# Context loads ahead of the row loads that wait, a slot's rows split ahead of its weight pieces with three homes for the transposes, and all slot loads issued by SyncE

## The reference, cut to what matters

```python
si = ctx @ W[:, :256][0];  sj = ctx @ W[:, 256:][0]          # per batch
xattn = 0.6 * sigmoid(si[:, :, None] + sj[:, None, :] + b) + 0.4 * layernorm(x)
x = x + tanh(g_xattn) * xattn
xt = layernorm(x).reshape(4096, 1024)
probs = softmax(xt @ wg);  e = argmax(probs);  gate = probs[e]
x = x + tanh(g_ffn) * gate * (xt @ W_ffn[e].T + b_ffn[e])     # one expert per token
```

## Time and profile before

| | |
|---|---|
| Median of 3 runs | 746.28 us (744.73 to 748.25) |
| The profiled execution: its own time, its span | 753.2 us, 751.5 us |
| TensorE, VectorE, GpSimd, ScalarE busy | 78%, 57%, 44%, 37% of the span |
| Granted TensorE clock, mean | 0.87 of full speed |
| First stage, until the last router product | 0 to about 222 us |
| Slot products, first to last | 259.8 to 737.9 us, 36 slots |
| DMA | 134.5 MB, 179 GB/s on average |

### The profile page before, as it was taken

How to read it: one execution, slowest core, us unless ns; L and a number is a source line. 1 busy time by engine, 2 the same in 40 slices (tenths; PEclk the granted TensorE clock), 3 DMA queues, 4 the chain that set the end, 5 groups by cost and what they waited for, 6 DMA issues and landing times.

```text
span 751.5 us, 13383 instructions
## 1 busy us (share of the span) xinstructions
PE 582.9 (78%) x2841; PEld 468.4 (62%) x2842; DVE 431.0 (57%) x555; ACT 275.6 (37%) x408; POOL 333.5 (44%) x488
## 2 busy tenths in 40 slices
PE   6798384668870199977977998797798799949992
PEld 5566263456660187856865887586587578738882
DVE  4377171538867887377278257457537735673341
ACT  3576243337741433233233233233324323332221
POOL 2467272637862333533533532532543254236552
PEclk9599586869995599988998999898899789979996
DMA  7803343516768886586586549648537745725552
GB/s 274 343 2 131 123 142 112 196 59 221 231 240 269 225 223 200 158 224 196 165 224 196 170 143 237 188 144 244 173 126 201 216 158 156 193 85 172 165 169 62
DMA packets 83718, 134.48 MB, mean 179 GB/s; under 512 B 11584, under 2 KB 64320, under 8 KB 83648
## 3 DMA queue, kind: packets, MB, share of 16 engines
q1 hardware_dynamic: 46496, 59.83, 27.5%
q10 hardware_dynamic: 27360, 40.17, 19.3%
q0 software_dynamic: 9792, 33.82, 11.3%
HBM read 99.97 MB, written 35.91 MB: 181 GB/s over the span
## 4 chain that ended last, share of the span: by engine, by line
issue 21%; PE 21%; DVE 20%; ACTq 10%; ACT 8%; DMA 7%; POOL 6%; DVEq 2%; SPq 2%; POOLq 2%
PE pair L970 9%; DVE wt L720 7%; ACT wt L532 4%; PE pair L897 3%; DVE pair L715 3%; PE pair L908 3%; DMA table<-xr,pos 3%; DMA ctx_in<-in_ctx 3%; ACTq L261 3%; DVE xr L656 3%; DVE rows L741 2%; PE pair L881 2%; DVE scatter_row L738 2%; PE pair L886 2%; ACTq L584 1%
## 5 line engine op out<-in xcount | busy, mean ns | idle before, releaser
L970 PE MATMUL pair<-wt,xt 128*128 x1728 | 421.8, 408 | 88.5 <-DVE xt L732 56.2
L970 PEld LDWEIGHTS pair<-wt,xt 128*128 128x128 f32 x1728 | 342.0, 199 | 168.0 <-issue 94.4
L424 POOL TENSOR_TENSOR rows<-rows,rb 128x1024 f32<-128x1024 f32 x37 | 88.1, 2382 | 185.0 <-ACT rb L551 185.0
L732 DVE TENSOR_TENSOR xt<-pair,xt 128x1024 fp32r<-128x1024 f32 x38 | 46.3, 1218 | 87.9 <-ACT xt L538 87.7
L532 ACT ACTIVATE wt<-pair 128x1024 f32 (+1 forms) x64 | 64.5, 1025 | 80.3 <-DVE pair L715 72.8
L715 DVE STREAM_TRANSPOSE pair<-w_raw 128x1024 f32<-128x1024 f32 x64 | 78.4, 1248 | 25.1 <-issue 24.0
L720 DVE TENSOR_TENSOR wt<-pair,wt 128x1024 f32 (+1 forms) x64 | 77.6, 1212 | 23.6 <-ACT wt L532 23.6
L538 ACT ACTIVATE xt<-pair 128x1024 fp32r<-128x1024 f32 x38 | 39.0, 1026 | 102.5 <-issue 49.8
L728 DVE STREAM_TRANSPOSE pair<-xb 128x1024 f32<-128x1024 f32 x38 | 47.8, 1259 | 44.2 <-issue 24.5
L551 ACT ACTIVATE rb<-bias_bc,scal 128x1024 f32 (+1 forms) x37 | 46.0, 1244 | 54.9 <-POOL scal L421 43.0
L908 PE MATMUL pair<-xc_tr,wg_sb 128*8 128x128 f32 x512 | 64.9, 283 | 0.0
(11 more groups left out here) (120 smaller groups left out, 452.9 us busy)
## 6 DMA issues: line engine op xcount, KB each, us to landing
w_raw<-in_L_ffn_W SPq DMA_DIRECT2D x256, 128.0 KB, 3.2
rows<-table ACTq DMA_DIRECT2D x38, 520.0 KB, 4.2
xb<-table ACTq DMA_DIRECT2D x152, 128.0 KB, 2.6
xr<-in_x SPq DMA_DIRECT2D x32, 512.0 KB, 6.0
ctx_in<-in_ctx SPq DMA_DIRECT2D x8, 512.0 KB, 4.7
bias_bc<-in_L_ffn_b SPq DMA_DIRECT2D x8, 512.0 KB, 4.4
out_x<-rows,scatter_row POOLq DMA_INDIRECT x36, 4.0
rows<-table SPq DMA_DIRECT2D x1, 520.0 KB, 5.5
```

The source lines that it names most:

```text
L424: nc.gpsimd.tensor_tensor(rows[:, k, 0:H], rows[:, k, 0:H], rb[:, :], ALU.add).then_inc(base_ready, 1)
L732: nc.vector.tensor_tensor(xt[:, k, 1, :, :].rearrange("p k n -> p (k n)"), ps[:, :], xt[:, k, 0, :, :].rearrange("p k n -> p (k n)").bitca ...
L970: last = nc.tensor.matmul(out_ps[r % 2][:, HALF * h:HALF * (h + 1)], xt[:, r % 2, x_part, k, :], wt[:, bass.ds(par, 1), w_part, k, HALF * ...
```

## The change

It has four parts. (1) SyncE issues context groups 4 to 7 ahead of all x tiles from 16 on. (2) In a slot, rows t + 2 are transposed first and cut behind the first piece's transpose, and the slot is finished last; `xt` has three homes. (3) SyncE issues all table loads and weight pieces in a loop of its own, and ScalarE none; `rows` has three buffers (`RING` = 3) and each loop is unrolled six times (`TURN` = 6), so `SLOTS` is 42. One number, `work`, tells what a slot does: 1 rows alone, 2 the first slot of an expert (pieces 0 to 3), 3 the slot behind it (pieces 4 to 7), 4 both. (4) Between the stages the order is new, and `finished` is raised early. The rest makes room in SBUF: `ones`, `after_start` and two others lie in tensors of the first stage. The core of the diff, in the order of the file: sizes, SyncE, ScalarE, VectorE between the stages, VectorE in a slot.

```diff
 
     Q, NB, QW = 4, 4, H // 4
...
-    RING = 4
...
-    TAB = SLOTS + RING
+
+    RING = 3
...
+            for g in range(4, NG):
+                sp.wait_ge(ctx_turned, g - 1)
+                sp.dma_start(ctx_in[:, g % 2, :], group_of(ctx_t, g)).then_inc(ctx_landed[g % 2], 16)
             for t in range(RX, T):
-                if t % GR == 0 and t // GR < NG:
-                    g = t // GR
-                    sp.wait_ge(ctx_turned, g - 1)
-                    sp.dma_start(ctx_in[:, g % 2, :], group_of(ctx_t, g)).then_inc(ctx_landed[g % 2], 16)
                 sp.wait_ge(row_stored[slot_of(t)], 16)
                 sp.dma_start(xr[:, slot_of(t), 0:H], tile_of(x_t, t)).then_inc(x_landed[slot_of(t)], 16)
...
-            load_rows(sp, 0, 0, 0)
-            for n in range(K, E * K):
-                e, m = n // K, n % K
-                sp.wait_ge(w_turned, n - WR + 1)
-                load_piece(e, m)
-                if m == WR:
-
-                    sp.wait_ge(w_ready, K * e + 1)
-                    sp.dma_start(bias_bc[:, e % 2, :], bias[e:e + 1, :].to_broadcast([P, H])).then_inc(bias_landed, 16)
+            load_blocks(sp, 0, 0)
+            load_rows(sp, 0, 0)
+            sp.wait_ge(slots_told, 1)
...
+            load_blocks(sp, row_of(1), 1)
+            load_rows(sp, row_of(1), 1)
+            sp.wait_ge(xb_turned, 1)
+            load_blocks(sp, row_of(2), 2)
+            for m in range(WR):
+                sp.wait_ge(w_turned, K - WR + m + 1)
+                load_piece(1, m)
+
+            with sp.Fori(0, SLOTS // TURN) as i:
+                for r in range(TURN):
+                    t = TURN * i + r
+                    work = sp.value_load(slot_tab[0:1, 0, bass.ds(t, 1)], min_val=0, max_val=4)
+                    with sp.If(work > 0):
+                        sp.wait_ge(xb_turned, t + 2)
+                        load_blocks(sp, row_of(t + 3), r + 3)
+                        if r == 0:
...
+                            sp.wait_ge(out_stored[(r - 1) % RING], 32 * i + 16 * ((r - 1) // RING + 1))
+                        load_rows(sp, row_of(t + 2), r + 2)
+                        with sp.If(work > 2):
+
+                            before = sp.value_load(slot_tab[0:1, 3, bass.ds(t, 1)], min_val=0, max_val=E - 2)
+                            with sp.If(before < E - 2):
+                                e = sp.value_load(slot_tab[0:1, 3, bass.ds(t, 1)], min_val=0, max_val=E - 3)
+                                for m in range(WR):
+                                    sp.wait_ge(w_turned, K * e + K + WR + m + 1)
+                                    load_piece(e + 2, m)
+                            with sp.Else():
+                                sp.nop()
+                            sp.nop()
+                        with sp.Else():
+                            sp.nop()
...
+                        with sp.If(work > 1):
+                            with sp.If(odd < 1):
+                                e = sp.value_load(slot_tab[0:1, 1, bass.ds(t, 1)], min_val=0, max_val=E - 2)
+                                for m in range(WR, K):
+                                    sp.wait_ge(w_turned, K * e + K + m - WR + 1)
+                                    load_piece(e + 1, m)
+
+                                sp.wait_ge(w_ready, K * e + K + 1)
+                                sp.dma_start(bias_bc[:, bass.ds((e + 1) % 2, 1), :].rearrange("p a h -> p (a h)"),
+                                             bias[bass.ds(e + 1, 1), :].to_broadcast([P, H])).then_inc(bias_landed, 16)
+                            with sp.Else():
...
-            next_rows(1, 1, 0)
-            xt_high(0, 0, cut_b)
             cut_high(0, 4, 0, cut_a)
             cut_high(0, 5, 0, pair[1])
-            exp_sum(0, 0)
+            xt_high(0, 0, cut_b)
             cut_high(0, 6, 0, cut_a)
             cut_high(0, 7, 0, pair[1])
+            exp_sum(0, 0)
             scaled_bias(0, 0, 0, 0)
...
+                    with act.If(work > 0):
+
+                        settled(summed, t + 1)
+                        xt_high(t + 2, (r + 2) % RING, cut_a)
                         exp_sum(t + 1, (r + 1) % RING)
-                    with act.Else():
-                        act.nop()
...
+                        with act.If(work > 2):
+                            last_pieces()
...
+                        odd = act.snap(work % 2)
+                        with act.If(work > 1):
+                            with act.If(odd < 1):
+                                first_pieces()
...
                         e1 = act.value_load(slot_tab[0:1, 1, bass.ds(t + 1, 1)], min_val=0, max_val=E - 1)
                         scaled_bias(t + 1, (r + 1) % RING, e1, act.snap(e1 % 2))
-                        next_rows(t + 3, (r + 3) % RING, i + (r + 3) // RING)
-                        settled(summed, t + 2)
-                        xt_high(t + 2, r, cut_a)
...
             position(NG - 1)
...
+            dve.sem_inc(finished, 2)
+            turn_weights(0, 2, cut_a, 2)
+            turn_weights(0, 3, pair[1], 3)
...
             cut_low(0, 3, 0, pair[1])
+            turn_weights(0, 4, cut_a, 4)
+            turn_weights(0, 5, pair[1], 5)
+            cut_low(0, 4, 0, cut_a)
             turn_rows(0, 0, 0, cut_b)
-            turn_weights(0, 4, cut_a)
+            cut_low(0, 5, 0, pair[1])
+            turn_weights(0, 6, cut_a, 6)
             xt_low(0, 0, cut_b)
-            turn_weights(0, 5, pair[1])
-            cut_low(0, 4, 0, cut_a)
...
             xt_low(1, 1, cut_b)
-
-            dve.sem_inc(finished, 2)
...
                         for m in range(first, first + K // 2):
-                            turn_weights(e, m, (cut_a, cut_b)[m % 2])
-                            if m > first:
-                                cut_low(e, m - 1, par, (cut_a, cut_b)[(m - 1) % 2])
-                        cut_low(e, first + K // 2 - 1, par, cut_b)
+                            turn_weights(e, m, (cut_b, cut_a)[m % 2], m - first)
+                            if m == first:
+                                behind_first()
+                            else:
+                                cut_low(e, m - 1, par, (cut_b, cut_a)[(m - 1) % 2])
+                        cut_low(e, first + K // 2 - 1, par, cut_a)
                         settled(w_ready, K * e + first + K // 2)
 
...
+                    def rows_cut(t=t, home=home):
+                        xt_low(t + 2, home, cut_a)
+                        dve.wait_ge(xt_ready, t + 3)
+
+                    with dve.If(work > 1):
+                        rows_turned()
+                        with dve.If(work > 2):
+                            last_pieces(rows_cut)
+                            with dve.If(work > 3):
+                                first_pieces(lambda: None)
+                            with dve.Else():
+                                dve.nop()
+                            dve.nop()
+                        with dve.Else():
+                            first_pieces(rows_cut)
+                        finish(t, r)
...
+                        with dve.If(work > 0):
+                            rows_turned()
+                            xt_low(t + 2, home, cut_a)
+                            finish(t, r)
```

More of the change, by code:

```diff
@@ L737, in finish @@
                 settled(base_ready, t + 1)
-                nc.vector.tensor_tensor(scatter_row[:, r:r + 1], rows[:, r, TOK:TOK + 1].bitcast(I32),
+                s = r % RING
+                nc.vector.tensor_tensor(scatter_row[:, s:s + 1], rows[:, s, TOK:TOK + 1].bitcast(I32),
                                         beyond[:, bass.ds(t, 1)], ALU.max)
                 settled(summed, t + 2)
-                nc.vector.scalar_tensor_tensor(out=rows[:, r, 0:H], in0=out_ps[r % 2][:, :], scalar=scal[:, r, 7:8],
-                                               in1=rows[:, r, 0:H], op0=ALU.mult, op1=ALU.add).then_inc(finished, 1)
-            turn_weights(0, 0, cut_a)
+                nc.vector.scalar_tensor_tensor(out=rows[:, s, 0:H], in0=out_ps[r % 2][:, :], scalar=scal[:, s, 7:8],
+                                               in1=rows[:, s, 0:H], op0=ALU.mult, op1=ALU.add).then_inc(finished, 1)
+            turn_weights(0, 0, cut_a, 0)
             for h in range(2):
                 dve.wait_ge(xc_copied[h], T)
-            turn_weights(0, 1, pair[1])
+            turn_weights(0, 1, pair[1], 1)
             cut_low(0, 0, 0, cut_a)
@@ L751, in _ @@
             position(NG - 1)
-            turn_weights(0, 2, cut_a)
-            turn_weights(0, 3, pair[1])
+            dve.sem_inc(finished, 2)
+            turn_weights(0, 2, cut_a, 2)
+            turn_weights(0, 3, pair[1], 3)
             cut_low(0, 2, 0, cut_a)
@@ L861, in _ @@
             for n in range(8):
-                nc.tensor.matmul(pair[1][:, 0:P], ones[:, :], ones[:, :], start=True, stop=True)
+                nc.tensor.matmul(pair[1][:, 0:P], ones, ones, start=True, stop=True)
             pe.wait_ge(masks_ready, 1)
```

(10 more changed lines are left out.)

222 lines of the change are left out of this document (117 added, 105 removed).

## The result

The changed kernel takes **689.05 us** (median of 4 runs, 688.07 to 693.0), the kernel before 747.08 beside it: a ratio of 0.9237, 95% interval 0.9193 to 0.928. In a second comparison on another chip, with the kernel before at 750.22, it took 687.3, ratio 0.9187 (0.9104 to 0.927). The forecast was 657, with a range of 628 to 692. The direction is right and the time is inside the range, but the gain is 58 us and not 89.

What follows compares the result with a forecast made beforehand. TensorE's waits for context loads and for `xt_low` behind VectorE's long turns, plus slow clock, bound it: 753.2 - 40 - 3 - 50.4 + 4 = 663.8 on the profiled execution, less 6.9 to the median: 657 us, range 628 to 692.

Steps and rivals of the forecast that it cites:

- code loading in every long turn: Rival: each of 12 long turns behind slot 3 costs 3 us more for instruction fetch; 693 us, chance 0.1.
- the rival with the port always lost: Slots: VectorE's finish always waits for GpSimd's addition, h = 18.1 us; 682 on the profiled execution, 675 us; chance 0.23.
- Part 1, tiles: Tile stage: TensorE's three waits for context loads go, with some slow products; -40 us, bounds -30 and -46.
- Part 2, passage: Between the stages: TensorE may start near 248 instead of 259.8 us, which brings little by itself.
- Part 3: Slots: one TensorE wait of 2.4 us per expert plus 2.0 slow clock; -50.4 us, first change another -3.
- h: Length of one long VectorE turn, a slot that prepares weights, from finish to finish; taken as 17 us.
- The dead heat at the port: In a long turn, row numbers and GpSimd's addition start together; h = 15.9 or 18.1 us, the middle, 17, taken.
- the rule of the Trainium skill: GpSimd and a two-SBUF-input VectorE operation share a port in turn; the later is blocked for the other's whole length.
- The low part of the rows now covers ScalarE's 1.3 us.: Long turn: VectorE's wait of 1.3 us for ScalarE ahead of the first cut is hidden behind the rows' low part.
- VectorE wins the port: Rival, slots: row numbers start before GpSimd's addition, h = 15.9 us, TensorE's wait shrinks to 0.2; 629 us, chance 0.2.
- Part 4, queues: ScalarE loses five DMAs a slot, hidden, nothing counted; SyncE's 21 issues make 9.5 us in a turn of 17.
- Part 5, loops: Returns to the loop's head in longer loops +3 us (0 to 6), two more empty slots at the end +1; +4.

Runs made afterwards that it cites:

- the context alone: The kernel before with only the context loads moved ahead, slots as before: 708.93 us, ratio 0.9438 to the kernel before.
- the run with the late count: The changed kernel with the count of finished slots raised late again, behind the setup of slots: 691.63 us, ratio 0.917 to the kernel before.
- the port alone: The changed kernel with VectorE's row-number operation moved from the turn's end to behind the rows' low part: 677.93 us, ratio 0.9035 to the kernel before.
- the kernel with the sum last: The changed kernel with ScalarE's exponent sum behind the high parts of the pieces instead of ahead of them: 671.47 us, ratio 0.8939 to the kernel before.
- the longer body: The changed kernel with 12 slots in the loop's body instead of 6, and 36 slots in all instead of 42: 678.21 us, ratio 0.9053.

## Why the prediction was right, and where it wasn't

**Sum against sum**, on the spans of the profiled executions, 751.5 and 687.3 us: -64.2, forecast -89.4. To slot 3: 296.73 to 252.94, -43.8 (forecast -40 - 3). Slots 3 to 30: 373.0 to 348.3, -24.7 (forecast -50.4, and +3 for the returns). The last six: 68.0 to 67.8. From the last product to the end: 13.7 to 18.3, +4.6 (forecast +1). So 22.7 of the 25 us of error are in the third stretch, slots 3 to 30, and 3.6 at the end. That 689 lies inside the range is partly luck: its upper end stood for code loading in every long turn (693 us), and the rival with the port always lost came to 675.

**Part 1, tiles: right.** -40 forecast; the last router product ended at 184.2 instead of 221.8, -37.6, with 5 us lost ahead of tile 4 (in the second profile at 180.8); with the context alone, the first slot product came 41.1 earlier. x tile 16 wasn't late.

**Part 2, passage: right.** First product forecast at 208, measured 211.2 and 207.2. That starting early brings little by itself is what the run with the late count showed.

**Part 3, the step that failed: the length of a long turn.** The formula held: wait = 1.3 + 2h - 32.9. The turns of t = 4 and 5, 13 and 14, 17 and 18, 22 and 23, 27 and 28 took 36.0, 36.1, 38.4, 35.2 and 36.7 us in pairs, which by the formula gives 4.4, 4.5, 6.8, 3.6 and 5.1; TensorE waited 4.86, 5.05, 7.12, 4.07 and 5.58. (The sixth pair, t = 8 and 9, 40.9 us, gave the two waits ahead of slots 10 and 11: 8.5 us together, by the formula 9.3.) But h was 18.6 on average, not 17, so waits were 35.2 us and not 14.4, and slow clock 16.9, not 12. In h three things were mis-sized.
- *The dead heat at the port.* I took the middle; GpSimd's addition won in 11 of 14 long turns (1.9 to 2.4 us for the row numbers), lost in 3 (0.16); in the second profile it was 12 and 2. Nothing lay between, as the rule of the Trainium skill that the prediction quotes has it. The heat isn't drawn afresh each time: both sides start from the same last high part, and the order comes out the same way in most turns. Out of the way, it gave 7 to 9 us in the slot stage.
- *"The low part of the rows now covers ScalarE's 1.3 us."* It did not, since ScalarE's exponent sum stands ahead of the piece's high part and waits for GpSimd: VectorE waited 1.0 to 3.8 us ahead of the first cut in 12 of the 14 long turns. That is why the three turns that won the port still took 17.6 to 18.8, and not 15.9; the rival "VectorE wins the port" couldn't have come true at 15.9. That the sum behind the pieces gave 0.8939 against 0.9035 for the port alone is in line with it, with some 6 to 7 us.
- *A gap that I carried over.* Take from the three won turns (t = 4, 13, 27) the waits ahead of the first cut (3.50, 3.00, 3.82 us) and for blocks (none, 0.39, 0.61), and 14.2 to 14.3 us are left, as in the kernel with the sum last (14.0 to 14.9), not 15.9. In the kernel before, t = 5 had a gap of 1.6 us ahead of the first weight transpose. It is still in my 15.9, and in no long turn of the changed kernel; 15.9 less 1.6 is 14.3:

```profile
336.41 2.39 DVE L715 STREAM_TRANSPOSE pair<-w_raw 128x1024 f32<-128x1024 f32 x2 [1.62 <-issue]
```

Over the twelve long turns behind slot 3 this adds up, on average: 14.4 us of work, 2.1 ahead of the first cut, 1.5 at the port, 0.5 for blocks and a return, 18.6 in all (14.4 is what is left when the measured waits are taken off). The first cut cost more than the port.

The rival "the port is lost always" (682 on the profiled execution) was nearest in its mechanism.

**Part 4, queues: not nothing.** ScalarE's issues were counted as hidden; handing four of them back, a slot earlier, cost 5 to 9 us (0.9305 against 0.9237 and 0.9187). And SyncE's load of the blocks, behind the weight pieces and a wait for a scatter, I didn't follow at all; my 9.5 us of issues "in 17" left out what they wait for: 19.7 us of waits on VectorE, 3.7 at the longest, one of them ahead of the long turn t = 8 that took 22.9 us.

**Part 5, loops: the place was wrong.** I counted ScalarE's gap at a return (4.5 us) and held VectorE's for small. VectorE's were 5.1 to 6.0 in four of five returns. With two returns instead of five the slot stage was 4.6 to 6.7 us shorter, so the five cost some 8 to 11 us (an estimate, from three returns' share). How much of that is more than the kernel before paid at its own returns isn't shown, so the +3 stays open. The +1 for the end was too low: it is 4.6 us, and with neither empty slots nor a return behind the last filled one the end fell from 18.1 to 11.6.

## What to carry to other kernels

When a chain runs through two engines twice per period, look for every instruction that stands ahead of the critical one on the *other* engine and waits for a third: here a tiny exponent sum, behind GpSimd's small numbers, held the first cut for 1.9 us in a long turn on average, more than the tie at the port (1.6). Two operations that are released by the same event and share a port need not split the wins evenly, and here they didn't (11 to 3); read the order out of the trace, and move the small one away from the large one, which cost nothing here. And once one engine's turn is mended, the next longest turn sets the pace: here the loop's returns, then the queue that issues all loads; add up each engine's turn with its waits before the change, not only that of the engine that is late now. When an edit of a loop also changes how many turns it runs empty, read the stage and the end apart: of the 9 us that the longer body gave, a large part came behind the last product.

## What the runs showed of the hardware that I had not expected

- A VectorE operation on 128x1 numbers that starts up to 0.5 us behind a GpSimd addition of 128x1024 takes 1.9 to 2.4 us instead of 0.15, in 11 of 14 meetings, and ends with it. In the other three it took 0.16; there both began within 0.01 us of each other, as in two of the eleven.
- VectorE stood still for 5.1 to 6.0 us at the loop's returns of the changed kernel, where its longest such gap before was 2.1 us; the loaded instructions went from 60 to 150 packets. With two returns instead of five it was 5.6 and 4.3 us at just two places (126 packets).
- The transpose of tile 4 started between 49.6 and 59.4 us over the profiled executions, at 59.33 and 54.13 in two of one and the same kernel. The spread lies ahead of anything that the experiments edit; its cause wasn't looked for.
